# A graph layer and a mixture of experts on one core: expert 0's split moved off GpSimd, the gates' store moved, routing spread over more steps, the split turns read from tables

## What is computed

```python
x = x + gnn(layernorm(x), edge_attr, node_vec, src, dst, W_self, W_func, W_att)
x = x + ffn(layernorm(x), router_w, w1, w2, w3)
# gnn: e = leaky_relu([z[src], z[dst], w] @ W_att.T); alpha = softmax of e over the edges of a dst
#      h_new = relu(h @ W_self.T + segment_sum(alpha * z[src], dst)); returns h + h_new
# ffn: gates = the two largest of softmax(x @ router_w.T), normalized to sum 1
#      out = sum over e of gates[:, e] * ((silu(x @ w1[e].T) * (x @ w3[e].T)) @ w2[e].T)
```

## Time and profile before

| | |
|---|---|
| median of 3 executions | 1061.29 us (1060.54 to 1061.91) |
| the profiled execution | 1062.78 us |
| its span, first to last instruction | 1061.0 us |
| TensorE busy | 845.9 us (80%) |
| VectorE busy | 648.2 us (61%) |
| GpSimd busy | 591.3 us (56%) |
| ScalarE busy | 449.6 us (42%) |
| mean granted clock of TensorE | 0.895 of full |
| GpSimd's gathers in the stream (L826) | 416, 0.957 us each |
| chain that ended last: TensorE, issue, VectorE, DMA | 29%, 5%, 4%, 3% |

### The profile page before, as it was taken

How to read it: one execution, slowest core, us unless ns; L and a number is a source line. 1 busy time by engine, 2 the same in 40 slices (tenths; PEclk the granted TensorE clock), 3 DMA queues, 4 the chain that set the end, 5 groups by cost and what they waited for, 6 DMA issues and landing times. The chain is left out here.

```text
span 1061.0 us, 18883 instructions
## 1 busy us (share of the span) xinstructions
PE 845.9 (80%) x4404; PEld 707.1 (67%) x4405; DVE 648.2 (61%) x2266; ACT 449.6 (42%) x1067; POOL 591.3 (56%) x558
## 2 busy tenths in 40 slices
PE   6955879866866667775688734799999999999995
PEld 6912445554655555664566633799999999999995
DVE  6634555655656696666676797356566565656553
ACT  4423243464465446556356811434344243443331
POOL 1177777777777777777775140634443544435332
PEclk9986989987888888898789956799999999999998
DMA  7776666565554455555454106442534422222221
GB/s 230 218 248 188 194 193 187 139 182 174 149 144 133 131 141 139 136 144 142 132 141 131 56 11 206 126 104 40 119 61 96 112 50 40 40 40 40 40 40 20
DMA packets 81157, 128.86 MB, mean 121 GB/s; under 512 B 21372, under 2 KB 56705, under 8 KB 80593
## 3 DMA queue, kind: packets, MB, share of 16 engines
q0 software_dynamic: 30720, 69.90, 28.2%
q1 hardware_dynamic: 43161, 51.59, 15.9%
q10 hardware_dynamic: 7200, 6.56, 1.8%
HBM read 106.86 MB, written 17.86 MB: 118 GB/s over the span
## 5 line engine op out<-in xcount | busy, mean ns | idle before, releaser
L826 POOL DMA_INDIRECT early<-ztab,early x416 | 398.1, 957 | 175.5 <-issue 172.8
L1347 PE MATMUL bank<-early,W 128*128 128x258 f32 x832 | 236.9, 438 | 14.3 <-DVE W L1846 11.5
L1411 PE MATMUL bank<-split_w,operands 128*128 x1344 | 237.6, 326 | 2.9 <-DVE operands L1984 1.4
L1411 PEld LDWEIGHTS bank<-split_w,operands 128*128 128x128 f32 x1344 | 213.4, 190 | 9.0 <-issue 6.7
L1347 PEld LDWEIGHTS bank<-early,W 128*128 128x128 f32 x832 | 174.2, 219 | 62.9 <-issue 30.9
L876 POOL DMA_INDIRECT xg<-ttab,slot_rows x56 | 55.5, 990 | 223.9 <-DVE late L2011 179.1
L1044 ACT ACTIVATE W<-early 128x128 f32<-128x128 f32 x208 | 91.0, 484 | 117.1 <-PE bank L1347 113.6
L1311 PE MATMUL bank<-ident,early 128*16 128x128 f32 x104 | 23.3, 368 | 128.2 <-DVE early L1829 128.2
L869 POOL DMA_INDIRECT out_rows<-late,slot_rows x56 | 88.9, 1588 | 32.8 <-issue 15.9
L1118 ACT ACTIVATE late<-bank 128x384 f32<-128x384 f32 x56 | 27.4, 490 | 183.8 <-PE bank L1411 183.7
L1311 PEld LDWEIGHTS bank<-ident,early 128*16 128x16 f32 x104 | 10.0, 117 | 140.2 <-DVE early L1829 137.8
(11 more groups left out here) (230 smaller groups left out, 1428.4 us busy)
## 6 DMA issues: line engine op xcount, KB each, us to landing
W<-in_wt SPq DMA_DIRECT2D x26, 512.0 KB, 4.4
W<-in_experts SPq DMA_DIRECT2D x40, 266.5 KB, 2.8
early<-ztab,early POOLq DMA_INDIRECT x416, 3.0
W<-in_experts SPq DMA_DIRECT2D x3, 2132.0 KB, 8.7
early<-in_x SPq DMA_DIRECT2D x26, 128.0 KB, 2.1
early<-ztab SPq DMA_DIRECT2D x25, 128.0 KB
early<-late SPq DMA_DIRECT2D x25, 128.0 KB
out_rows<-early ACTq DMA_DIRECT2D x25, 128.0 KB, 1.9
```

The lines of the kernel that those rows point to most:

```text
L826: nc.gpsimd.indirect_dma_start(out=zg[:, k * KG + c, :], out_offset=None, in_=ztab, in_offset=bass.IndirectOffsetOnAxis(ap=src_here[:, k / ...
L1347: last = mm(ps[2 + k // 2 % 2][:, 0:ZR], prob_hot[:, k % 3, c * P:(c + 1) * P], zg[:, k * KG + c, :], start=(k % 2 == 0 and c == 0), stop= ...
L1411: last = mm(bank[:, 0:n], x[:, (k % 2 * KC + c) * P:(k % 2 * KC + c + 1) * P], split_w[:, bass.ds(at + (part + w + c * H), n)], start=(i = ...
```

## The change

- GpSimd's `split_first` is gone. ScalarE makes the high part of expert 0 after the last exponential of the routing; VectorE makes the low part, piece 0 before the slots, piece 1 in turn 0, at the start of a new function `split_turns`. TensorE waits for piece 1 only ahead of slot 0's down product.
- `gates_store` is called before SP's loads of experts 1 and 2. The gates lie in another region of memory.
- `early_route` covers 13 steps: the prefix sums are at i = 2, the rank product at i = 6 and in `ps[5]`, its reader at i = 7, one-hots from i = 8. TensorE's wait for the readers moves from `node_parts` to the mirror product.
- Tile 24's stages run at step 93 plus the lag, not 96, and its router products use `ps[0]`.
- `split_next` is replaced by three tables, `split_act`, `split_both` and `slot_done`, made in `split_turns` after the first token's low part. ScalarE waits for them at turn 2, GpSimd ahead of its first split. An expert with one or two slots is split sooner; with three or more in the same turns as before. On VectorE `lo_piece` now stands behind `gated`.

```diff
@@ GpSimd, and ScalarE in its place
-                pool.wait_ge(sums_psum, GROUPS)
-                split_first(pool)
+                act.wait_ge(experts_in[0], 16)
+                act.wait_ge(sums_psum, GROUPS)
+                split_hi(act, 0)
                 keep_tokens()
@@ SP
-                sp.wait_ge(stream_over, 1)
+                gates_store()
                 for e in range(len(EXPERTS_AFTER), RAW):
                     expert_load(e)
@@ tiles
             def at_group(t, k, r):
+                if t == LAST_AT:
+                    stage(TILES - 1, (TILES - 1) % NODE_RING, (TILES - 1) // NODE_RING)
                 j = r * NODE_RING + k // BATCH
-                if k % BATCH or (isinstance(j, int) and j >= TILES):
+                if k % BATCH or j >= TILES - 1:
                     return
@@ TensorE, routing
-                    if i == 2:
+                    if i == 6:
+                        pe.wait_ge(top_ready, min(ROUTES[b][1] + 8, GROUPS // BATCH))
                         rank_of(b)
-                    elif b is not None and 5 <= i < 5 + CHUNKS_OF[b]:
-                        tokens_of(b, i - 5)
+                    elif b is not None and i >= 9:
+                        tokens_of(b, i - 9)
@@ TensorE, mirror product
                     pe.wait_ge(back_ready, batch(k, r) + 1)
+                    for b, (lo, hi) in enumerate(ROUTES[:-1]):
+                        if batch(k, r) == hi + 8:
+                            pe.wait_ge(choice_ready, 3 * b + 3)
@@ VectorE, routing
                     elif i == 2:
-                        ranks_of(b)
+                        prefix_of(b)
                     elif i == 3:
                         gates_of(b)
-                    elif b is not None and i < 4 + CHUNKS_OF[b]:
-                        one_hots(b, i - 4)
+                    elif i == 7:
+                        ranks_of(b)
+                    elif b is not None and 8 <= i < 8 + CHUNKS_OF[b]:
+                        one_hots(b, i - 8)
@@ VectorE, slots
+            split_lo(dve, v, 0, 0)
+
+            def split_turns():
+                split_lo(dve, v, 0, 1)
+                v.memset(changes, 0.0)
...
+                link(v.tensor_scalar(behind_f, exp_f, 1.0, None, ALU.add))
+                v.scalar_tensor_tensor(behind_f, exp_f, float(E - 1), behind_f, ALU.is_lt, ALU.mult)
+                link(v.tensor_tensor(changes[:, 1:SLOTS], exp_f[:, 1:SLOTS], exp_f[:, 0:SLOTS - 1], ALU.subtract))
+                link(v.tensor_tensor(after_all, changes[:, 0:SLOTS], behind_f, ALU.mult))
+                link(v.tensor_tensor(after_1, after_all, changes[:, 1:SLOTS + 1], ALU.mult))
+                link(v.tensor_tensor(longer, after_all, after_1, ALU.subtract))
...
+                v.tensor_copy(split_act[0:1, :], for_act[0:1, 0:SLOTS])
+                v.tensor_copy(slot_done[0:1, :], for_done[0:1, 0:SLOTS])
+                v.tensor_copy(split_both[0:1, :], for_dve[0:1, 0:SLOTS]).then_inc(expert_ready, 1)
+                dve.wait_ge(expert_ready, 2)
@@ in xT_low
+                if isinstance(t, int) and t == 0:
+                    split_turns()
@@ VectorE's order of a turn
-            run(dve, SLOTS, RING, 1, [(1, hid_first), (2, hidT_low), (0, xT_low), (1, hid_second), (3, lo_piece),
-                                      (2, gated)])
+            run(dve, SLOTS, RING, 1, [(1, hid_first), (2, hidT_low), (0, xT_low), (1, hid_second), (2, gated),
+                                      (0, lo_piece)])
```

More of the change, by code:

```diff
@@ L84 @@
 EXPERTS_AFTER = (44,)
+LAST_AT = BATCH * (TILES - 2) + 1
 PEEL = GROUPS // AHEAD
@@ L89 @@
 ROUTE_RING = 2
+RANK_AT = 2 * BC
 CHUNK = 3
@@ L200, in build @@
         iota_h, o = carve(ef, o, [2 * P], fp16)
+        gates, o = carve(ef, o, [TILES, E])
         assert o <= 5 * WE
@@ L552, in split_lo @@
                 .then_inc(lo_split[piece], 1)
[L554 to L564, removed]
         def chunk_no(b, i):
@@ L580, in early_route, with split_named @@
                 i = t - BATCH * (hi - 1)
-                if 0 <= i < 5 + CHUNKS_OF[b]:
+                if 0 <= i < 9 + CHUNKS_OF[b]:
                     return b, i
             return None, None
[L585 to L590, removed]
+        def split_named(eng, table, t, work):
+            e = eng.value_load(table[0:1, bass.ds(t, 1)], min_val=0, max_val=E - 1)
             with eng.If(e > 0):
-                eng.wait_ge(y_psum, t)
                 work(e)
@@ L624, in tiled, with router_bank @@
             return at_group
+        def router_bank(j):
+            return ps[0] if j == TILES - 1 else ps[7]
         def uses(k):
@@ L1101, in hi_parts @@
             def hi_parts(t, k, r):
+                if isinstance(t, int) and t < 2:
+                    return
+                if isinstance(t, int) and t == 2:
+                    act.wait_ge(expert_ready, 2)
                 def work(e):
+                    act.wait_ge(y_psum, act.value_load(slot_done[0:1, bass.ds(t, 1)], min_val=1, max_val=SLOTS))
                     act.wait_ge(raw_in, e + 1)
                     split_hi(act, e)
-                at_new_expert(act, t, work)
+                split_named(act, split_act, t, work)
             def xT_copy(t, k, r):
@@ L1421, in up_first @@
                 pe.wait_ge(xT_lo_ready, t + 1)
-                for piece in range(2):
-                    pe.wait_ge(lo_split[piece], e + 1)
+                pe.wait_ge(lo_split[0], e + 1)
                 if at_least(t, 1):
+                    pe.wait_ge(lo_split[1], e + 1)
                     pe.wait_ge(hid_a_ready, t)
@@ L1447, in down @@
                     pe.wait_ge(y_ready, t)
+                else:
+                    pe.wait_ge(lo_split[1], 1)
                 def high(i):
```

100 lines of the change are left out of this document (61 added, 39 removed).

## The result

The changed kernel took 1070.84 us in the median (1068.93 to 1071.66), the kernel before 1061.6 beside it: ratio 1.0084, 95% interval 1.0066 to 1.0103. It is **slower by 0.8%**, outside the range (1043 to 1061) and on the side to which I gave a chance of 0.08. The profiled execution took 1068.93 us, with a span of 1067.2 (before 1062.78 and 1061.0).

The account below looks back on a forecast made before the run. The expert slots were taken as bound by TensorE, worth only what keeps it from waiting. −4.0 − 15.4 − 1.1 − 1.2 + 7.7 + 2.1 + 5.4 = −6.5 gave 1054.8, said as 1055 us; range 1043 to 1061.

Parts of the forecast that it names:

- The batches over 13 steps: Edge stream: rank product and reader moved later, both 5.2 us VectorE waits and two gather gaps go; −4.0 us.
- Expert 0 off GpSimd: Stream's end: four VectorE instructions no longer wait out GpSimd's split and fall back to 0.21 us each; −15.4 us.
- The table in slot 0: Slot 0: table's two-input VectorE operations wait out GpSimd's low part of expert 1; +7.7 us, plus 2.1 for the clock.
- table not held: Rival in slot 0: GpSimd late or its instruction does not lock, last two slot 0 terms go; 1045 us, chance 0.22.
- batches not spread: Rival in the edge stream: mirror product's new wait stops TensorE, neither gaps nor tail improve; 1059.5 us, chance 0.12.
- The order of VectorE and the turns in the slots: Split turns: low piece behind gated output delays the last low part, +0.9 us for each of six experts; +5.4 us.
- the piece starts near 819.4: Split turn at 817.84: low piece starts right behind the two gated output instructions and ends near 822.5; +0.9 us.
- ScalarE's and GpSimd's turns are where they were: Slots: for experts of three slots or more, these engines' split turns stay unchanged; no cost added.
- The rival that ended slower: Split turns: whole low piece on TensorE's path, 6 x 3.12 = 18.7 us instead of 5.4; 1068 us, chance 0.08.
- Tile 24: Stream's tail: interleaving tiles 23 and 24 runs their chains side by side, VectorE's queue then limits; −1.1 us.
- Gates ahead of the loads: End of routing: early gates release GpSimd 2.2 us sooner, but the first gather flies inside a load; −1.2 us.
- the first low piece on VectorE: Before slot 0: expert 0's piece, 3.12 us, fits between the tables' end and the first token's low part; nothing.

Follow-up runs that it names:

- run 4: Changed kernel with GpSimd waiting for the table of split turns before its low part of expert 1; ratio 0.9982 to the kernel before.
- run 6: Changed kernel with no ScalarE load of or wait on `slot_done`, low piece ahead of gated output, GpSimd's first split behind the table; 1047.21 us.
- Run 2: Changed kernel with VectorE's low piece back ahead of the gated output; ratio 0.9971 to the kernel before.
- Run 1: Changed kernel without ScalarE's load of `slot_done` and its wait on it ahead of a high split; ratio 1.0028 to the kernel before.
- run 7: Changed kernel with the loads of experts 1 and 2 sent at the stream's end, gates' store behind them; ratio 1.0074 to the kernel before.
- run 8: Changed kernel with the gates' store back behind the loads of experts 1 and 2; ratio 1.0072 to the kernel before.
- run 9: Edits of run 6 and run 7 together on the changed kernel; 1044.75 us, ratio 0.9826 to the kernel before.
- run 3: Changed kernel with the table of split turns made at the end of the routing, right behind `expert_of`; ratio 1.0005 to the kernel before.
- run 5: Changed kernel with tile 24 back at its old step, a whole batch behind tile 23; ratio 1.0068 to the kernel before.
- run 10: Kernel of run 9 with expert 0's first low piece moved ahead of the routing's last memset; ratio 0.9840 to the kernel before.

## Why the prediction was wrong

**Right.** The batches over 13 steps: no gap between gathers over 1.6 us, no wait for the rank product in the stream, 5.0 us where I had 4.0. Expert 0 off GpSimd: the four VectorE instructions of the earlier trace rows take 0.17 to 0.21 us, which is the 15.4 us. The table in slot 0: 8.0 for 7.7, and the clock 1.9 for 2.1 (twelve products in 4.20 us after the pause, where twelve took 2.34 just before it). Runs 4 and 6 show that mechanism to be the whole of it. The rival "table not held" is out. L1986 is a one-input operation, and I had counted on two-input ones alone, though the earlier trace rows show a one-input copy held as well; by the Trainium skill ("SBUF — State Buffer", Who interferes with whom) a tensor_scalar can enter a two-port mode and then contends with GpSimd, and its 5.98 us agree.

The rival of batches not spread is out too: nothing in the stream waits for the mirror product's new wait.

**Wrong: the sum.** It was off by 12.7 us: 7.3 in the slots, 3.4 in the tail and 2.9 on the way to slot 0, less 1.5 by which the stream was better, and 0.7 in small things.

*The order of VectorE and the turns in the slots* (+5.4, measured +12.7). In the step to "the piece starts near 819.4" I set the piece right behind the two instructions. The register load and the branch ahead of it had been hidden in the wait for TensorE, and once the piece came behind that wait they cost 0.91 to 1.08 us each time. Run 2 prices the order at 10.1 us, above my upper bound of 8. And "ScalarE's and GpSimd's turns are where they were" failed for ScalarE: the turn is the same, but the split starts later in it, because it now reads `slot_done` as well, and I put that at nothing. Run 1 prices it at 3.6. Both undone give 11.9 of the 12.7. The rival that ended slower put the whole piece of 3.12 us on the path; that is not what happened (6 x 3.12 = 18.7 against 10.1), but its place, TensorE's wait for the last low part, was the right one. That its time, 1068, is the nearest to the measured one is luck: the rest came from places that it did not name.

*Tile 24* (−1.1, measured about +2). By the stretches, the tail of 43.89 less 15.4 is 28.5; with the interleaving it is 31.2 on average, without it 29.1. So the interleaving costs 2.2 us (in the changed kernel itself 1.7). The 0.6 that is left would be the later rank product with its one-hots; no run tried that alone. I had seen that one-hots would stand in tile 24's way. They stand in tile 23's way too: in the changed kernel both tiles' statistics wait behind them, and then both logits come last:

```profile
618.24 0.18 DVE L1625 BATCH_NORM_AGGREGATE early<-early 128x2 f32<-128x6 f32 x1 [0.16 <-DVE early L1620]
...
621.43 0.16 DVE L1629 RECIPROCAL early<-early 128x1 f32<-128x1 f32 x1
...
625.92 0.17 DVE L1638 COPY logits<-bank 128x8 f32<-128x8 f32 x1 [2.55 <-PE bank L1257]
627.48 0.17 DVE L1638 COPY logits<-bank 128x8 f32<-128x8 f32 x1 [1.39 <-PE bank L1257]
```

Between the first two lines stand twelve one-hots of other tiles, 0.26 to 0.30 us each. That order is read from the timeline; which of the instructions costs how much was not tried one by one.

*Gates ahead of the loads* (−1.2, measured +1.7; −0.6 with the loads out of the way, run 7). The gather's release came 2.1 us sooner, where I had 2.2. The bound for its flight, "landing between 665.6 and 667.1", was right too: it was 2 us longer under the loads. What failed was the first low piece on VectorE, which I put at "nothing". It was to start at the end of the tables; it started 4.88 us later, and slot 0's low part of the tokens waits for its end. In the kernel before such an idle time could not be seen: its first instruction behind the branch, L1984, waited for ScalarE's copy in any case (5.08 us).

## What to carry to other kernels

An operation that is moved takes its register load and branch with it: look for what idle time hid those two, not only the operation. A wait on a value from a table costs the reading of the table even when its condition has long been met (0.6 us in a turn here), so it is to be priced before it is put at nothing. And VectorE's small work beside a whole GpSimd elementwise instruction is best reordered at the source (one wait on GpSimd gave back 9.9 us), since moving the victim away only hands the hold to the next one.

## What the runs showed of the hardware

**VectorE's entry into code behind a branch.** The first instruction behind it waited 2.6 to 2.8 us where the two expert loads were over (runs 7, 8, 9), 2.3 in run 3, where VectorE came to it 14.0 us after the loads were issued (10.3 in the changed kernel) and found them running out, and 4.7 to 4.9 us where it came while they ran at a DMA share of 0.8 to 1 (changed kernel, runs 1, 2, 4, 5, 6). Under an instruction of 3.1 us it did not show (run 10). It is no wait for something that the piece needs: in run 10 the same piece ran right behind the table of experts. Nor is it the row gather, beside whose landing the piece starts in most of these runs: in run 8 it started 1.3 us before the first product on the gathered rows, in run 3 1.6 us after it. The list of DMA queues in that window, 640 to 656, of the changed kernel (packets, MB, share of 16 engines):

```profile
q1 hardware_dynamic: 256, 2.76, 42.9%
q0 software_dynamic: 192, 0.54, 11.0%
q8 instruction: 3, 0.05, 1.1%
q14 instruction: 6, 0.05, 0.8%
```

The two queues named instruction have shares of the same 16 engines that carry the loads. That VectorE waits for a fetch of instructions fits all the runs; no row ties one packet to VectorE, so it stays the likely cause.

**VectorE's two-input operation holds GpSimd's indirect DMA.** An output add that starts 0.49 us after the start of a piece of 3.12 us takes 4.10 us in place of 1.59, and a gather 3.11 in place of 0.94 (run 8). In all six split turns of the changed kernel the add ends 1.46 to 1.47 us after the piece does, so nearly all of its own time is spent behind it. The Trainium skill ("SBUF — State Buffer", Who interferes with whom) reports a probe in which a tensor_copy stalled a DMA and a tensor_tensor did not, and infers that a tensor_tensor leaves descriptor writing free; of a GpSimd instruction that reads SBUF the same section says that two SBUF inputs on VectorE do contend with it. The piece is a tensor_tensor of fp32 with both inputs in SBUF, and the measurement decides: it holds an indirect DMA. These DMAs take their row numbers from `slot_rows` in SBUF, so it may be GpSimd's reading that waits and not its writing; no run separates the two. The other way round there was nothing: in run 3 the table's two-input operations took at most 0.25 us while the gathers were being issued.
